# Narrow jobs' scores from four row groups in float32, issued once per job, in the fused four-layer cross-attention kernel

## The reference

```python
def narrow(x, cond, wq, wk, wv, wo, norm_w):          # layers 0 and 3
    xn = rmsnorm(x, norm_w)
    q = (xn @ wq).reshape(B, T, 16, 8); k = (cond @ wk).reshape(B, S, 4, 8); v = (cond @ wv).reshape(B, S, 4, 8)
    scores = einsum('btgrd,bsgd->bgrts', q.reshape(B, T, 4, 4, 8), k) / sqrt(8)
    out = einsum('bgrts,bsgd->btgrd', softmax(scores), v).reshape(B, T, 128)
    return x + out @ wo
def wide(x, cond, Wq, Wk, Wv, Wo, bo, ...):           # layers 1 and 2
    q = x @ Wq; k = cond @ Wk; v = cond @ Wv          # 16 heads of 64
    probs = softmax(q k^T / 8 + col_bias)
    return (probs v) @ Wo + bo + x
```

## Time and profile before

| | |
|---|---|
| median of 3 runs | 380.88 us (380.61 to 384.76) |
| profiled execution, its own time | 380.89 us |
| its span, first to last instruction | 379.10 us |
| mean granted TensorE clock | 0.986 |
| busy: PE / DVE / ACT / POOL | 95% / 71% / 74% / 49% |
| chain that ended last | PE 74%, DVE 21%, ACT 3% |

### The profile page before, as it was taken

The page is one execution under the profiler, slowest core; times in us unless marked ns, Lnnn a source line. Parts: engine busy times, 40 slices in busy tenths (PEclk is TensorE's granted clock), DMA queues, the critical chain, the costliest instruction groups (busy, mean ns, idle before and its releaser), DMA issues.

```text
span 379.1 us, 10494 instructions
## 1 busy us (share of the span) xinstructions
PE 359.7 (95%) x3522; PEld 319.1 (84%) x3522; DVE 267.7 (71%) x1401; ACT 279.0 (74%) x1176; POOL 187.6 (49%) x220
## 2 busy tenths in 40 slices
PE   8889999999999999999999999999999999978665
PEld 8787799899999998889889988888999989867554
DVE  2999975636536547696978886577564785699982
ACT  4889998865665567475899999998566865647793
POOL 3677853733223236454676765443333435447662
PEclk9899999999999999999999999999999999999979
DMA  7925000000000000000000000000000000000000
GB/s 232 411 66 216 1 3 3 2 3 2 1 2 3 2 0 3 2 3 0 10 3 9 9 8 2 3 3 2 0 3 2 3 2 1 2 3 3 7 9 14
DMA packets 4883, 9.91 MB, mean 26 GB/s; under 512 B 608, under 2 KB 3296, under 8 KB 4576
## 3 DMA queue, kind: packets, MB, share of 16 engines
q1 hardware_dynamic: 4400, 8.91, 6.5%
q10 hardware_dynamic: 432, 0.34, 0.4%
HBM read 8.73 MB, written 0.52 MB: 24 GB/s over the span
## 4 chain that ended last, share of the span: by engine, by line
PE 74%; DVE 21%; ACT 3%; issue 1%; DVEq 0%; POOL 0%; POOLq 0%
PE pt_ps L849 13%; PE scores_ps L836 9%; DVE probs L615 8%; PE q_ps L796 8%; PE fill_ps L701 7%; PE v_ps L900 7%; PE v_ps L882 7%; PE fill_ps L702 7%; PE fill_ps L703 7%; PE v_ps L870 3%; DVE probsT L626 3%; ACT probs L482 3%; PE q_ps L788 2%; DVE qn L598 2%; DVE qn L594 2%; PE scores_ps L825 2%
## 5 line engine op out<-in xcount | busy, mean ns | idle before, releaser
L482 ACT ACTIVATE probs<-probs,negmax 128x128 f32<-128x128 f32 x512 | 198.5, 391 | 81.0 <-DVE negmax L615 80.9
L379 POOL TENSOR_TENSOR probs<-probs,inv 128x512 f32<-128x512 f32 x128 | 137.3, 1075 | 176.8 <-DVE inv L622 176.4
L482 ACT ACTIVATION_READ_ACCUMULATOR probs<-probs,negmax 128x1 f32 x512 | 96.8, 189 | 0.0
L615 DVE CUSTOM_DVE_ANT_0 probs<-scores_ps,col_bias 128x128 f32<-128x128 f32 x256 | 58.2, 284 | 39.1 <-PE scores_ps L836 39.1
L849 PE MATMUL pt_ps<-smalls,probs 128*128 128x128 f32 x512 | 70.5, 282 | 6.2 <-DVE probsT L626 6.2
L849 PEld LDWEIGHTS pt_ps<-smalls,probs 128*128 128x128 f32 x512 | 57.6, 143 | 18.2 <-issue 14.8
L615 DVE CUSTOM_DVE_ANT_0 probs<-scores_ps,no_bias,inv_rms 128x128 f32<-128x128 f32 x224 | 64.2, 343 | 5.8 <-PE scores_ps L825 5.4
L626 DVE COPY probsT<-pt_ps 128x512 f32<-128x512 f32 x96 | 63.0, 684 | 2.6 <-PE pt_ps L849 0.5
L615 DVE DVE_READ_ACCUMULATOR2_ANT negmax<- 128x1 f32 x512 | 42.5, 83 | 0.0
L701 PE MATMUL fill_ps<-c_hi,w_hi 128*128 128x256 f32 x128 | 38.3, 300 | 0.0
L836 PE MATMUL scores_ps<-kT,qT 64*128 64x128 f32 x512 | 37.2, 285 | 0.0
(11 more groups left out here) (92 smaller groups left out, 583.2 us busy)
## 6 DMA issues: line engine op xcount, KB each, us to landing
kT<-in_kv_w SPq DMA_DIRECT2D x6, 512.0 KB, 6.4
w_qo<-in_qo_w SPq DMA_DIRECT2D x2, 1024.0 KB, 8.3
v<-in_ctxT SPq DMA_DIRECT2D x4, 256.0 KB, 9.5
v<-in_kv_w SPq DMA_DIRECT2D x2, 512.0 KB, 11.2
outT<-x SPq DMA_DIRECT2D x8, 64.0 KB, 1.6
wn<-in_narrow_w SPq DMA_DIRECT2D x2, 192.0 KB, 5.7
x<-in_xT SPq DMA_DIRECT2D x1, 384.0 KB, 8.1
oT<-in_narrow_kv ACTq DMA_DIRECT2D x1, 256.0 KB, 3.9
```

The source lines that it names most:

```text
L379: nc.gpsimd.tensor_tensor(p4, p4, inv[:, o % 2, side, :].unsqueeze(2).broadcast_to([P, 4, S]), ALU.mult,).then_inc(probs_made[side], 1)
L482: last = nc.scalar.activation(e, e, ACT.Exp, scale=-1.0, bias=negmax[:, o % 2, side, q:q + 1], accum_out=rowsum[:, o % 2, side, q:q + 1])
L615: last = nc.vector.tensor_tensor_reduce(out=probs[:, o % PROBS_RING, side, cols], in0=banks[scores_bank(o)][side][:, cols], in1=bias, scal ...
```

## The change

A narrow job's queries are made by one product of 128 x 128 (`narrow_queries`, into `qn_ps`, a part of the bank `v_ps`) and kept in float32: the rows r*32 to r*32+31 are the 32 channels of the r-th head of each group. The keys are kept four times below each other in float32 (`kn`, no splitting, weights four times instead of three), so `kd` has 128 rows. Four float32 products of 32 rows x 512 columns, one on each row group of the array, give all four banks of the job at once: `scores_ps0`, `scores_ps1`, `fill_ps0`, `fill_ps1` (called A0, A1, B0, B1). Half h = 1 of a narrow job has no scores on PE. In the half that has them the transposes stand ahead of them. Since four banks hold scores, fills take turns over A0, A1, B0, B1 and the query bank Q0 by a table; in the first half of a narrow job the fill stands in A0, in the second in A1 and Q0. Some fills move to the half after. ACT copies the A1 fill ahead of the second exponentials where the next job is narrow (`soon`).

```diff
-    30: ["v4.1", "v4.2"], 31: ["v4.3"], 32: ["k5.0", "k5.1"], 33: ["k5.2"], 34: ["k5.3", "v5.0"], 35: ["v5.1"],
-    36: ["v5.2", "v5.3"], 37: ["k6.0"], 38: ["k6.1", "k6.2"], 39: ["k6.3", "v6.0"],
+    7: [("k1.1", A0), ("k1.2", B0)],
+    24: [("v3.3", A0)], 25: [("k4.0", A1), ("kn2.0", Q0)], 26: [("k4.1", A0)], 27: [("k4.2", A1), ("vn3", Q0)],
+    36: [("v5.2", A0)], 37: [("v5.3", A1), ("k6.0", Q0)], 38: [("k6.1", A0)], 39: [("k6.2", A1), ("k6.3", B0)],
+    40: [("v6.0", B1)], 41: [("v6.1", B0)], 43: [("kn2.3", B1), ("v6.2", B0)], 44: [("v6.3", B1)], 45: [("k7.0", B0)],
...
+            def free_bank(bank, use):
+                if count_of(bank, use) > 1:
+                    pe.wait_ge(bank_read[bank], count_of(bank, use) - 1)
...
-                    for r in range(REP):
-                        first = NQ + (NARROW.index(l) * REP + r) * STACK
-                        last = nc.tensor.matmul(q_ps[0:STACK, r * T:(r + 1) * T], wn[:, first:first + STACK], x[:, b, :],
-                                                start=True, stop=True)
+            def narrow_queries(n):
+                l, b = job(n)
+                if n >= 3:
+                    pe.wait_ge(v_read, uses(n - 3, 1))
...
+                nc.tensor.matmul(ms_ps, x_sq[:, n % 2, :], mean_w[:, 0:2], start=True, stop=True).then_inc(ms_full, 1)
...
+                nc.tensor.matmul(qn_ps, wn[:, first:first + C], x[:, b, :], start=True, stop=True).then_inc(qn_full, 1)
...
+            def narrow_scores(n):
+                i = narrow_index(n)
+                for r in range(REP):
+                    free_bank(r, (2 * n + r // 2, r % 2))
+                pe.wait_ge(kd_made, i + 1)
+                pe.wait_ge(qn_made, i + 1)
+                for r in range(REP):
+                    rows = slice(PART * r, PART * (r + 1))
+                    nc.tensor.matmul(banks[r][:], qn[rows, n % 2, :], kd[rows, i % KD_RING].rearrange("p g k -> p (g k)"),
+                                     start=True, stop=True).then_inc(bank_full[r], 1)
...
                 if is_narrow((o + 4) // 2):
                     pe.wait_ge(rms_out, narrow_index((o + 4) // 2) + 1)
+                    pe.wait_ge(qn_made, narrow_index((o + 4) // 2) + 1)
...
-                if valid(o):
-                    scores(n, h)
+                if is_wide(n):
+                    wide_scores(n, h)
...
                 if valid(o - 2):
                     transpose_probs(o - 2)
+                if is_narrow(n) and h == 0:
+                    narrow_scores(n)
...
                 if h == 1 and is_narrow(n + 1):
                     mean_out(n + 1)
+                    narrow_queries(n + 1)
```

More of the change, by code:

```diff
@@ L130, in uses, with scores_bank, bank_uses, count_of @@
     return sum(2 if is_wide(m) else 1 for m in range(n)) + (h + 1 if is_wide(n) else 1)
[L133 to L145, removed]
+def scores_bank(o, side):
+    return 2 * (o % 2) + side if is_narrow(o // 2) else side
+def bank_uses():
+    order = [[] for _ in range(5)]
+    for o in range(-1, 2 * NJOBS):
+        n, h = o // 2, o % 2
+        octets = [o, o + 1] if is_narrow(n) and h == 0 else [] if is_narrow(n) or o < 0 else [o]
+        for octet in octets:
+            for side in range(2):
+                order[scores_bank(octet, side)].append((octet, side))
+        for name, bank in FILLS.get(o, []):
+            order[bank].append(name)
+        if o >= 0 and is_wide(n + 1):
+            order[Q0].append(("queries", n + 1, h))
+    return order
+BANK_USES = bank_uses()
+def count_of(bank, use):
+    return BANK_USES[bank].index(use) + 1
 def narrow_index(n):
@@ L491, in half @@
                     wide_queries(n + 1, 0)
-                for name in FILLS.get(o - 1, [])[1:]:
+                for name, bank in FILLS.get(o - 1, [])[1:]:
                     if name != "bias":
@@ L499, in half @@
                     nc.scalar.activation(probsT[:, (o - 2) % PROBST_RING, 1, :], pt_ps[1][:], ACT.Copy).then_inc(pt_read[1], 1)
+                soon = h == 1 and is_narrow(n + 1)
+                for name, bank in FILLS.get(o, [])[:1]:
+                    if soon:
+                        fill_out(name)
                 if valid(o):
                     exponentials(o, 1)
-                for name in FILLS.get(o, [])[:1]:
-                    fill_out(name)
+                for name, bank in FILLS.get(o, [])[:1]:
+                    if not soon:
+                        fill_out(name)
                 if o in (0, 1):
@@ L611, in scores_out @@
                     dve.wait_ge(rms_made, narrow_index(n) + 1)
-                dve.wait_ge(scores_full[side], o + 1)
+                if l in NARROW and h == 1 and side == 0 and o >= 3:
+                    for i in range(2):
+                        dve.wait_ge(pt_full[i], o - 2)
+                bank = scores_bank(o, side)
+                dve.wait_ge(bank_full[bank], count_of(bank, (o, side)))
                 for q in range(4):
@@ L660, in half @@
                     outputs_out((o - 3) // 2, (o - 3) % 2)
-                for m in NARROW_JOBS:
-                    if m > 0 and query_half(m) == o - 1:
-                        narrow_queries(m)
                 if valid(o - 2):
@@ L742, in project_context @@
                     pe.wait_ge(narrow_lo, 1)
-                    last = three(out[0:STACK, 0:PAIR], [narrow_parts(NK + (n * CC + c) * STACK, STACK) for c in range(CC)],
+                    last = three(out[:, 0:PAIR], [narrow_parts(NK + (n * CC + c) * P, P) for c in range(CC)],
                                  [(c_hi[:, p, c, :], c_lo[:, p, c, :]) for c in range(CC)])
@@ L810, in scores, with wide_scores @@
+            def wide_scores(n, h):
                 o = 2 * n + h
                 l, b = job(n)
[L812 to L827 removed]
@@ L828, in scores @@
-                pe.wait_ge(q_read, uses(n, h))
+                for side in range(2):
+                    free_bank(side, (o, side))
+                pe.wait_ge(bank_read[Q0], count_of(Q0, ("queries", n, h)))
                 f = WIDE_ROWS.index((b // 2, l))
                 for m in (2 * h, 2 * h + 1):
-                    pe.wait_ge(fill_read[fill_bank(f"k{f}.{m}")], fill_count(f"k{f}.{m}"))
+                    name = f"k{f}.{m}"
+                    pe.wait_ge(bank_read[FILL_BANK[name]], count_of(FILL_BANK[name], name))
@@ L835, in scores @@
                         rows = slice(side * WIDE_D, (side + 1) * WIDE_D)
-                        last = nc.tensor.matmul(out[side][:, c * S:(c + 1) * S], qT[rows, 4 * h + c, :],
+                        last = nc.tensor.matmul(banks[side][:, c * S:(c + 1) * S], qT[rows, 4 * h + c, :],
                                                 kT[rows, f % KV_RING, 4 * h + c, b % 2 * S:(b % 2 + 1) * S],
@@ L839, in scores @@
                         if c == 3:
-                            last.then_inc(scores_full[side], 1)
+                            last.then_inc(bank_full[side], 1)
             def transpose_probs(o):
```

205 lines of the change are left out of this document (77 added, 128 removed), and 9 rows, old and new, of the table FILLS.

## The result

The changed kernel takes 401.04 us (median of 4 runs, 398.91 to 402.0), the kernel before 381.28 in the same comparison: ratio 1.050, with a 95% interval of 1.046 to 1.054. It is slower, as forecast, but by 20 us and not by 5, and outside the range. The profiled execution took 402.0 us, its span 400.2, against 379.1 before.

A forecast was written before the change was run, and what follows sets the result against it. PE was taken to bound the wide and middle narrow stages, DVE the last; -0.75 + 2.55 + 2.8 + 0.2 + 0.6 = +5.4 on 380.89 gave 386.3 us, range 377.5 to 391.5.

The forecast's parts named there:

- The head: Start to half 8: keys ready sooner, DVE's query pieces gone, PE's scores of half 8 at 53.05 instead of 53.81; -0.75 us.
- The half-8 bank wait: Half 8: PE's wide scores wait for ACT's copy of k1.1, forecast to be reached near 53.0 us.
- The middle: Halves 24 to 40: entry, narrow loop, then late bank copy and v6.0 at half 40; +2.55 us together.
- Entry: Halves 24 to 28: product behind wv and transposes, A0 fills waiting 1.35 each, less work removed; S(27) +1.45 us.
- The loop: Middle narrow jobs: 9.2 us a job against 9.44 to 9.55 before; jobs 29 to 39 gain 1.8, S(39) level.
- side 1's transposes 0.44: Middle loop: after ACT's copy at t+7.4 and 0.14, only side 1's transposes, 0.44 us, then 0.1 and the product's 1.1.
- The last stage: From half 54: S(59) +2.8, narrow loop +0.2, last job +0.6 us, as jobs after wide ones get 2.3 longer.
- 0.14, 0.44, 0.1 and 1.1: Between DVE's last copy and next reduction: reaction, side 1's transposes, changeover, product; 1.8 us of DVE idleness once a job.
- half clock: Rival, last stage: PE's 3 us idle times lower the clock, slow jobs 29 to 31 cost +2 to +6, 388 to 392; 13%.
- The prediction's own sign: Forecast wrong if the clock is low for more than the 6.8 us that 20 us at 0.83 stand for.
- The transposes are not in the way: Rival: ACT and POOL run ahead, DVE idles below 1.1 us before S(2n,0), loop is PE's 8.9; 373 to 377 us; 15%.
- Pairs that don't overlap: Rival on the four-group product: only pairs overlap, 1.96 us in all 16 jobs, 398 us; one after another, over 415; 5%.

The follow-up runs named there:

- early_copy: front_last with ScalarE's copies of k1.1 and k6.2 ahead of its second exponentials in halves 7 and 39; 384.38 us, ratio 1.010.
- front_last: The changed kernel with the product of four row groups back in front of wide values and transposes in jobs 28 to 31 alone; 387.06 us, ratio 1.013.
- late_values: front_ends with projections v7.2 and v7.3 moved from halves 54 and 55 to 56 and 57; 380.19 us, ratio 0.996.
- late_one: front_ends with v7.2 moved from half 54 to 55 and v7.3 from 55 to 56, both in Q0; 379.33 us, ratio 0.995.
- busy_last: The changed kernel with idle products (4 and 8 per half) added on PE in halves 56 to 63; 394.71 us, ratio 1.033.
- pairs_last: The changed kernel with, in jobs 28 to 31, the product cut in two, two row groups in front of each half; 387.61 us, ratio 1.015.
- before_busy: The kernel before with 4 idle products in front of the transposes of octets 54 to 63; 382.43 us, ratio 1.004.
- front_ends: early_copy with the product in front of the transposes in jobs 12 and 13 too; 380.41 us, ratio 0.998.
- front_busy: front_last with 3 and 5 idle products per half in halves 56 to 63; 386.46 us, ratio 1.014.

## Why the prediction was wrong

**Right.** The direction, and that the order turns savings into waits. The product within 1.2 us (1.05 in the chain); PE stalls of 1.35 before the A0 fill (1.36 at half 26); the entry up to S(24) (+1.3 forecast, +1.36 measured); the bank at half 40 (1.15 forecast; PE idle 1.36 before the scores at 245.82, and 1.49 less in early_copy) and v6.0 behind it (0.96 left for 1.4); 41-54 unchanged.

**The head, -0.75 forecast, +1.85 measured.** The half-8 bank wait, which I let vanish because ScalarE would reach the copy near 53.0, was there (PE idle 1.36, copy at 54.95). And S(0) comes late in this one profile: at 12.35, where the forecast had 10.35 and front_last has 10.85. Without either the forecast would have been near: front_last has +0.22 with the wait, early_copy -1.08 without it. This has some luck in it, since late_values and late_one, with the same code up to S(8) as early_copy, have +1.10 and +0.24.

**The middle, +2.55 forecast, +4.6 measured.** Entry: S(27) was put at +1.45 and came at +2.21. The forecast has no term for PE's wait before the wide values of half 25 (0.97 us at 169.94, for DVE's mean; 0.31 in the kernel before), which is most of the difference. The loop was to win 1.45 back by S(39), at 9.2 us a job; it is 9.41 (202.29 to 211.70 on DVE's timeline, both first sides), no faster than before. The step that failed is "side 1's transposes 0.44". PE's own fills, and not ScalarE's copy (forecast 7.4 us behind the first side), release the transposes: they end 7.24 us behind the first side of half 30 (198.22), both sides are due by then, and the chain of the kernel after has them with 0.96 in front of the product:
```profile
205.22 0.23 PE q_ps L682
205.46 0.96 PE pt_ps L827 x8
206.42 0.63 PE scores_ps L797 x2
```
PE's work alone is near the 8.9 that I had put (39.68 us busy in 42, so about 0.5 idle in 9.41).

**The last stage, +3.6 forecast, +14.6 measured.** This is the error. S(57) to S(58) was to take 6.0 and took 9.32. The idle time of DVE between its last copy and its next reduction was put at 1.8 us: "0.14, 0.44, 0.1 and 1.1". The chain has 0.24 + 1.09 + 1.85 + 1.86 + 0.09 = 5.13 there: the wide octet's weighted values (1.09) were left out, though they stand ahead of the transposes and wait for the same copies; both sides are transposed, not one (1.02 for 0.44 at full clock, as the chain has it in half 56, at 339.44); and transposes and product ran at half clock (0.8 more each). S(56) to S(57), 6.0 forecast, took 7.59, all of the difference in mean square, query product and y projection at half clock (4.06 against 2.41). So the half clock was no separate rival of 13%, +2 to +6, but part of the forecast's own mechanism, since a loop in which PE and DVE wait for each other leaves PE idle 3 us at a time. I had the idle time in the text and priced it only for jobs 29 to 31, and only on transposes and product. The prediction's own sign for it came true: it called itself wrong if the clock were low for more than 6.8 us, and 0.85 over the 34 us from 340 on stands for 10.2 us at half clock. busy_last puts what it is worth at 6.3 us; 9.0 behind S(54) are the order at full clock (with what the idle products themselves delay); front_last shows that both go together.

The tail also lost 1.84 us. The granted clock from S(63) to the end is 0.84 there, and 0.99 in the kernel before. The two kernels with idle products and the changed product, 0.94 and 1.00, lose only 0.52 and 0.15; the others with the changed product have 0.74 to 0.88 and lose 1.32 to 2.04. That the half clock is the cause is argued from this, and not its size: the loss does not follow the clock step by step (pairs_last, 0.74, loses 1.72). before_busy has 1.92 more there at 1.00, for its own products.

One reading in the prediction is wrong without harm: the transposes are not recorded in two passes, eight of them leave eight records. The 0.11 us a record, and with it the 0.88 for one product of 512 columns in two passes, stay as an estimate; no run has one such product by itself.

**The rivals.** "The transposes are not in the way" is refuted by DVE's timeline at S(56), S(58) and S(60), where 1.1 was the point of decision (S(62) has 3.88):
```profile
341.66 0.35 DVE L597 CUSTOM_DVE_ANT_0 probs<-scores_ps,no_bias,inv_rms 128x128 f32<-128x128 f32 x1 [3.48 <-PE scores_ps L797]
...
358.57 0.35 DVE L597 CUSTOM_DVE_ANT_0 probs<-scores_ps,no_bias,inv_rms 128x128 f32<-128x128 f32 x1 [5.12 <-PE scores_ps L797]
...
371.57 0.35 DVE L597 CUSTOM_DVE_ANT_0 probs<-scores_ps,no_bias,inv_rms 128x128 f32<-128x128 f32 x1 [2.27 <-PE scores_ps L797]
```
Pairs that don't overlap are refuted by the 1.05. Was the rest of the change worth anything? A little: with the order mended at both ends and ScalarE's two copies moved, the same product, banks and query product are level with the kernel before (front_ends, 0.998, 0.995 to 1.000), and late_one, which has two fills moved back by a half too, is ahead by 0.2 to 0.7%. The new order alone, in four jobs, costs the old kernel 21 us.

## To carry to other kernels

When an instruction moves behind others in an in-order queue, list everything that now stands between its consumer's last input and it, down to what the first of them waits for, and price each piece twice, at full clock and at half. In the loop here, in which two engines took turns, PE stood idle 3 us at a time, and the clock took its share too, about 6 of the 14.6 us. And one order need not serve all stages: here the product belongs in front where VectorE is awaited, and behind the transposes where a late bank copy is.

## What the runs showed of the hardware

- Four float32 products of 32 rows on four row groups, 512 columns each, two passes: all four overlap (their records begin within 0.02 us), 1.05 us in the chain at full clock and 1.86 at half, against 0.94 for four products of 96 rows, two by two, before. Against an estimated 4 x 0.88 one after another that is 3.4 times as fast in the chain, and 3.1 times by the whole span of the records, 1.14 us (half 30, 196.95 to 198.09). The Trainium skill (TensorE: Matmul & The Clock Gate, Measured speedup vs the span model) gives 3.07 times for four row tiles of 512 columns; the span agrees with it.
- PE's busy share does not tell the clock: from 340 to 366 late_one is busy 16.50 of 26 us at a clock of 1.00, front_ends 18.95 at 0.87. Part of the larger share is the half clock itself, at which the same products take longer. Why one run keeps the clock there and the other not stays open.
- Idle products cost as well as help: before_busy, at a granted clock of 1.00 from S(54) to the end, is 0.4% slower than the kernel before, which is at 0.83 from 350 to 370.
- The head of the same code varied by 1.65 us between five profiles (kernel after to pairs_last and front_busy) and by 2.18 between four (early_copy, front_ends, late_values, late_one). A clock of 0.83 from 30 to 40 us goes with 1.1 to 1.6 us more from S(4) to S(5). The stretches between S(8) and S(54) repeat within 0.1.
